# Routed token rows of a mixture layer: a gather by a token table in place of a scatter in sorted order

## What is computed

```python
logits = xf @ gate_w.T                      # xf: 2048 normalized tokens x 512
probs = softmax(logits, axis=-1)            # 8 experts
topk_p, topk_i = top_k(probs, 2)
comb = (one_hot(topk_i, 8) * topk_p[..., None]).sum(axis=1)
h = silu(einsum('nc,eic->eni', xf, w1)) * einsum('nc,eic->eni', xf, w2)
eo = einsum('eni,eci->enc', h, w3)          # 352 hidden features per expert
y = einsum('enc,ne->nc', eo, comb)
sh = silu(xf @ sw1.T) * (xf @ sw2.T) @ sw3.T    # shared expert, 704 hidden
x = x + y + sh
```

## Time and profile before

| | us |
|---|---|
| timed runs, median of 3 | 1809.57 |
| timed runs, lowest and highest | 1806.09 and 1809.67 |
| the profiled execution, first to last instruction (span) | 1828.4 |
| the profiled execution's own time with what lies around the span | not listed |

### The profile page before, as it was taken

The page is one execution under the profiler, slowest core; times in us unless marked ns, Lnnn a source line. Parts: engine busy times, 40 slices in busy tenths (PEclk is TensorE's granted clock), DMA queues, the critical chain, the costliest instruction groups (busy, mean ns, idle before and its releaser), DMA issues.

```text
span 1828.4 us, 26550 instructions
## 1 busy us (share of the span) xinstructions
PE 1714.7 (94%) x9753; PEld 1320.4 (72%) x9753; DVE 1210.7 (66%) x2477; ACT 917.2 (50%) x1937; POOL 183.6 (10%) x299
## 2 busy tenths in 40 slices
PE   5899999999999999998999999998995999999998
PEld 4788888888888888875533333333894999999997
DVE  6665766666655666667689999995541256666756
ACT  2544444444444444332477787877420146666641
POOL 1000000000000000020122322221106000000025
PEclk8999999999999999997799999999897999999999
DMA  4000000010000000022133344442104067887836
GB/s 150 1 1 12 24 24 1 1 35 1 24 1 24 12 24 1 1 59 68 45 96 89 123 141 134 132 135 66 50 13 184 1 231 266 299 273 275 294 122 228
DMA packets 103204, 167.21 MB, mean 91 GB/s; under 512 B 8325, under 2 KB 52357, under 8 KB 102309
## 3 DMA queue, kind: packets, MB, share of 16 engines
q1 hardware_dynamic: 97956, 148.74, 25.3%
q0 software_dynamic: 5120, 16.78, 2.7%
HBM read 116.15 MB, written 49.28 MB: 90 GB/s over the span
## 4 chain that ended last, share of the span: by engine, by line
PE 77%; DVE 16%; issue 3%; ACT 2%; another core or an unknown queue 1%; POOL 1%; DMA 0%; POOLq 0%; DVEq 0%; ACTq 0%
PE ps L189 38%; DVE xmax L1768 9%; PE ps L195 8%; PE ps L1436 7%; PE ps L1239 7%; PE ps L1131 6%; PE ps L1321 4%; PE ps L1192 3%; PE ps L1311 2%; DVE stats L206 1%; PE ps L1372 1%; DVE al L1783 1%; PE ps L1129 1%; ACT ah L1541 1%
## 5 line engine op out<-in xcount | busy, mean ns | idle before, releaser
L1768 DVE TENSOR_REDUCE xmax<-ps 128x1 f32<-128x512 f32 x512 | 320.7, 682 | 36.1 <-PE ps L1192 35.4
L1563 ACT ACTIVATE xp<-ps 128x512 f32<-128x512 f32 x512 | 273.1, 602 | 93.5 <-PE ps L1311 92.5
L1496 ACT ACTIVATE probs<-ps,nmax 128x128 f32<-128x128 f32 (+3 forms) x256 | 136.2, 532 | 164.5 <-DVE nmax L1736 164.5
L1192 PE MATMUL ps<-k,q 48*128 48x512 f32 x512 | 207.3, 483 | 7.4 <-DVE xmax L1768 4.7
L1311 PE MATMUL ps<-q,k 50*128 50x512 f32 x512 | 196.9, 467 | 6.0 <-ACT xp L1563 6.0
L1192 PEld LDWEIGHTS ps<-k,q 48*128 48x128 f32 x512 | 86.7, 193 | 144.7 <-DVE xmax L1768 115.0
L1536 ACT CAST pth<-ps 128x128 fp32r<-128x128 f32 (+3 forms) x256 | 108.5, 424 | 87.7 <-PE ps L195 87.7
L1321 PE MATMUL ps<-xp,vx 128*32 128x512 f32 x1024 | 140.3, 622 | 0.8 <-issue 0.8
L1736 DVE TENSOR_REDUCE nmax<-ps 128x1 f32<-128x128 f32 (+3 forms) x256 | 123.4, 482 | 14.9 <-PE ps L1131 13.5
L189 PE MATMUL ps<-w12h,x_h 128*128 128x352 f32 x568 | 121.6, 336 | 10.8 <-issue 10.3
L1775 DVE TENSOR_TENSOR ptl<-ps,pth 128x128 fp32r<-128x128 f32 (+3 forms) x256 | 123.8, 484 | 2.0 <-ACT pth L1536 2.0
(11 more groups left out here) (191 smaller groups left out, 3527.1 us busy)
## 6 DMA issues: line engine op xcount, KB each, us to landing
w_raw<-in_w_t SPq DMA_DIRECT2D x56, 704.0 KB, 5.9
w_raw<-in_w_t SPq DMA_DIRECT2D x28, 768.0 KB, 5.9
q<-q_way SPq DMA_DIRECT2D x64, 192.0 KB, 3.1
rows_x<-w_raw SPq DMA_DIRECT2D x39, 256.0 KB, 3.3
mixed<-rows_x SPq DMA_DIRECT2D x39, 256.0 KB, 4.3
rows_y<-y_s SPq DMA_DIRECT2D x39, 256.0 KB, 5.5
q_way<-q_hi SPq DMA_DIRECT2D x32, 256.0 KB, 4.2
w_raw<-in_w_qkv_t SPq DMA_DIRECT2D x24, 256.0 KB, 2.9
```

Source lines behind the costliest of these rows:

```text
L1192: pe.matmul(ps[:, bank, :], q3[rows, m % 4, h // 2, i * P:(i + 1) * P].bitcast(F32R), k3[rows, m % KV, :].bitcast(F32R), start=True, stop= ...
L1496: act.activation(probs[u % 4][:, 0:w], ps[:, S_BANK + u % 2, 0:w], ACT.Exp, bias=nmax[:, u % 4:u % 4 + 1], accum_out=rsum[:, u % 4:u % 4 + ...
L1563: act.activation(xp[:, m % 2, h, t, :], ps[:, XST + n % 3, :], ACT.Exp, scale=X_SCALE).then_inc(s_xe, 1)
L1768: dve.tensor_reduce(xmax[:, m % 2, h % 2, h // 2, i:i + 1], ps[:, bank, :], AX_X, ALU.max, negate=True).then_inc(s_xmax, 1)
```

## The change

The scatter goes, and with it `rows_x`, the blanking on SP, the memset on POOL and the semaphores between them. Instead:

- SP stores the 16 tiles of `fn_all` plainly to `rows_n` in DRAM, in token order (`keep_normal`), each after its normalization and spaced by the steps of PE.
- `places` also splits each sorted row number into its tile (number / 128) and its row in the tile (number mod 128), as floats.
- `row_ones` (DVE, in step 7) makes from these two kinds of one-hots: `tile_hot`, 128 x 16 x 40 for each pick, and `row_hot`, 128 x 16 x 128 for each pick. POOL multiplies `tile_hot` by the token numbers. They lie where `y_s`, `fn` and `mixed` lie later.
- `whose_rows` (PE, at the end of step 8) adds 32 products of them into one bank: the token number of each of the 4992 sorted rows, 0 for a row that no token has. DVE copies it as integers in step 9 (`whose_row`).
- POOL gathers each routed tile from `rows_n` into `mixed` by that table (39 indirect DMAs), each once the tile four places ahead has been turned.

The gather at the end and the output are the same.

```diff
@@ SP
-            def take_rows(q):
-                if q >= 4:
-                    sp.wait_ge(s_ft, HEAD_TILES + q - 4 + 1)
-                sp.dma_start(mixed[:, q % 4, :], rows_x[row_of(q):row_of(q) + P, :]).then_inc(s_xr[q % 4], 16)
...
-            def blank(q):
-                if q == 0:
-                    sp.wait_ge(s_zero, 1)
-                sp.dma_start(rows_x[q * P:(q + 1) * P, :], w3_raw[0][:, 0, :]).then_inc(s_blank, 16)
+            def keep_normal(t):
+                sp.wait_ge(s_fn, t + 1)
+                if t >= 2:
+                    sp.wait_ge(s_h1, t // 2)
+                sp.dma_start(rows_n[t * P:(t + 1) * P, :], fn_all[:, t, :]).then_inc(s_kept, 16)
...
             for which in range(3):
                 load_piece(which, 1)
+            for t in range(TILES):
+                keep_normal(t)
             sp.wait_ge(s_tab, 1)
-            sp.wait_ge(s_sort, 16 * TOP * TILES)
-            for q in range(2):
-                take_rows(q)
+            sp.wait_ge(s_kept, 16 * TILES)
             sp.wait_ge(s_ft, HEAD_TILES)
@@ POOL
+            pool.wait_ge(s_ids, 4)
+            for r in range(TOP):
+                pool.wait_ge(s_thot, r + 1)
+                pool.tensor_tensor(tile_hot[:, r], tile_hot[:, r].bitcast(F32),
+                                   tok_f[:, :].unsqueeze(2).to_broadcast([P, TILES, N_WHOSE]), ALU.mult)\
+                    .then_inc(s_tok, 1)
-            pool.wait_ge(s_place, 1)
-            pool.wait_ge(s_blank, 16 * N_ROUTED)
-            pool.wait_ge(s_fn, TILES)
-            for t in range(TILES):
-                for r in range(TOP):
-                    pool.indirect_dma_start(rows_x, bass.IndirectOffsetOnAxis(ap=place[:, r, t:t + 1], axis=0),
-                                            fn_all[:, t, :], None).then_inc(s_sort, 16)
+            pool.wait_ge(s_idx, 1)
+            pool.wait_ge(s_kept, 16 * TILES)
+            for q in range(N_ROUTED):
+                if q >= 4:
+                    pool.wait_ge(s_ft, HEAD_TILES + q - 4 + 1)
+                at = row_of(q) // P
+                pool.indirect_dma_start(mixed[:, q % 4, :], None, rows_n,
+                                        bass.IndirectOffsetOnAxis(ap=whose[:, at:at + 1], axis=0))\
+                    .then_inc(s_xr[q % 4], 16)
@@ PE
+            def whose_rows():
+                pe.wait_ge(s_rhot, TOP)
+                pe.wait_ge(s_tok, TOP)
+                ins = products(pe, whose_ps, [(row_hot[:, r, t, :], tile_hot[:, r, t, :])
+                                              for r in range(TOP) for t in range(TILES)])
+                ins.then_inc(s_who, 1)
...
                 if i == RANK_STEP:
                     ranks()
+                if i == RANK_STEP + 2:
+                    whose_rows()
@@ DVE
-                dve.tensor_copy(place[:, :, :], place_f[:, :, :]).then_inc(s_place, 1)
+                count.seal(dve, dve.tensor_copy(place[:, :, :], place_f[:, :, :]))
+                count.mark(dve.tensor_scalar(part_i[:, 0], place[:, :, :], P - 1, None, ALU.bitwise_and))
+                count.seal(dve, dve.tensor_scalar(part_i[:, 1], place[:, :, :], P.bit_length() - 1, None,
+                                                  ALU.logical_shift_right))
+                dve.tensor_copy(part_f[:, :, :, :], part_i[:, :, :, :]).then_inc(s_row, 1)
+            def row_ones():
+                square, tall = [P, TILES, P], [P, TILES, N_WHOSE]
+                dve.wait_ge(s_ids, 4)
+                dve.wait_ge(s_row, 1)
+                for r in range(TOP):
+                    dve.tensor_tensor(tile_hot[:, r], part_f[:, 1, r, :].unsqueeze(2).to_broadcast(tall),
+                                      steps_f[:, 0:N_WHOSE].unsqueeze(1).to_broadcast(tall), ALU.is_equal)\
+                        .then_inc(s_thot, 1)
+                for r in range(TOP):
+                    dve.tensor_tensor(row_hot[:, r], part_f[:, 0, r, :].unsqueeze(2).to_broadcast(square),
+                                      steps_f[:, :].unsqueeze(1).to_broadcast(square), ALU.is_equal).then_inc(s_rhot, 1)
+            def whose_row():
+                dve.wait_ge(s_who, 1)
+                dve.tensor_copy(whose[:, :], whose_ps).then_inc(s_idx, 1)
...
                 if i == RANK_STEP:
                     places()
+                if i == RANK_STEP + 1:
+                    row_ones()
                 if i == RANK_STEP + 2:
                     slots()
+                if i == RANK_STEP + 3:
+                    whose_row()
```

More of the change, by code:

```diff
@@ L325 @@
 SORTED = N_ROUTED * P
+N_WHOSE = N_ROUTED + N_ROUTED % 2
 THRESHOLDS = BATCH * SEQ // BIG
@@ L338, with row_of @@
 COLUMN = {s: n for n, s in enumerate(BIG_AT + SMALL_AT)}
+def row_of(q):
+    s = FFN[X_FIRST[HEAD_TILES + q]].load - 2
+    col, second = COLUMN[s], q - tiles_of(s)[0]
+    return col * BIG + second * P if col < N_BIG else N_BIG * BIG + (col - N_BIG) * P
 Step = namedtuple("Step", "x load y opens closes")
@@ L522, in build @@
         s_lb = sem("s_lb")
-        s_zero = sem("s_zero")
-        s_blank = sem("s_blank")
         s_num = sem("s_num")
+        s_ids = sem("s_ids")
+        s_kept = sem("s_kept")
+        s_row = sem("s_row")
+        s_rhot = sem("s_rhot")
+        s_thot = sem("s_thot")
+        s_tok = sem("s_tok")
+        s_who = sem("s_who")
+        s_idx = sem("s_idx")
         s_pick = sem("s_pick")
         s_rank = sem("s_rank")
-        s_place = sem("s_place")
         s_tab = sem("s_tab")
-        s_sort = sem("s_sort")
         s_xr = [sem(f"s_xr{n}") for n in range(4)]
@@ L649, in build @@
         xg = sbc("xg", [P, 2, KC, P])
+        with ExitStack() as come:
+            tile_hot = come.enter_context(nc.sbuf_tensor("tile_hot", [P, TOP, TILES, N_WHOSE], F32R))
         y_s = sbc("y_s", [P, Y_RING, HID])
         fn = sbc("fn", [P, TAIL_TILES, HID])
+        with ExitStack() as come:
+            row_hot = come.enter_context(nc.sbuf_tensor("row_hot", [P, TOP, TILES, P], F32R))
         mixed = sbc("mixed", [P, 8, HID])
@@ L689, in build @@
         gate_s = sbc("gate_s", [P, KC, EXPERTS])
+        steps_i = sbc("steps_i", [P, P], mybir.dt.int32)
+        steps_f = sbc("steps_f", [P, P])
+        tok_i = sbc("tok_i", [P, TILES], mybir.dt.int32)
+        tok_f = sbc("tok_f", [P, TILES])
+        part_i = sbc("part_i", [P, 2, TOP, TILES], mybir.dt.int32)
+        part_f = sbc("part_f", [P, 2, TOP, TILES])
+        whose = sbc("whose", [P, N_WHOSE], mybir.dt.int32)
         weights_1 = block_of_weights(1)
@@ L697, in build @@
         rank_ps = ps[:, RANK, 0:EXPERTS * (TILES + 1)]
-        rows_x = nc.dram_tensor("rows_x", (SORTED, HID), F32).ap()
+        whose_ps = ps[:, RANK, 2 * P:2 * P + N_WHOSE]
+        rows_n = nc.dram_tensor("rows_n", (BATCH * SEQ, HID), F32).ap()
         rows_y = nc.dram_tensor("rows_y", (SORTED, HID), F32).ap()
@@ L867, in _ @@
                             context(n + 1)
-                for q in (2 * (m - KV - 1), 2 * (m - KV - 1) + 1):
-                    if 0 <= q < N_ROUTED:
-                        blank(q)
                 if m >= ITEMS - 2:
                     load_piece(m - (ITEMS - 2), 0)
-            sp.wait_ge(s_blank, 16 * N_ROUTED)
             load_piece(2, 0)
@@ L886, in _ @@
                 load_piece(which, 2)
-            for q in range(2, 4):
-                take_rows(q)
             for i in range(N_FFN + 2):
-                for q in range(4, N_ROUTED):
-                    if X_FIRST[HEAD_TILES + q - 4] == i + 1:
-                        take_rows(q)
                 for load in range(RING, N_LOAD):
@@ L1021, in cross @@
                 b, kv = m // KV, m % KV
-                if m == KV:
-                    pool.wait_ge(s_res, GROUPS * TILES + 1)
-                    pool.memset(w3_raw[0][:, 0, :], 0.0).then_inc(s_zero, 1)
                 if m + 1 < ITEMS:
@@ L1054, in _ @@
             power(BATCH - 1, 3 * BATCH)
+            pool.iota(steps_i[:, :], pattern=[[1, P]], base=0, channel_multiplier=0).then_inc(s_ids, 1)
+            pool.iota(tok_i[:, :], pattern=[[P, TILES]], base=0, channel_multiplier=1).then_inc(s_ids, 1)
+            pool.wait_ge(s_ids, 2)
+            pool.tensor_copy(steps_f[:, :], steps_i[:, :]).then_inc(s_ids, 1)
+            pool.tensor_copy(tok_f[:, :], tok_i[:, :]).then_inc(s_ids, 1)
             pool.iota(num_i[:, :], pattern=[[1, N_BIG]], base=0, channel_multiplier=0).then_inc(s_num, 1)
```

## The result

The changed kernel takes 1820.94 us in the median of 5 runs (1819.72 to 1822.43), the kernel before 1809.57 us (1797.03 to 1811.37). The ratio is 1.0084, 95% interval 1.0057 to 1.011: slower, by more than forecast and outside the range.

What follows compares the result with a forecast made beforehand. TensorE was taken to set the time from the feed-forward part on. Slip 0.1, wait 1.3 and matmuls 3.3 sum to 4.7 us, added to 1809.6 for 1814.3 us; the range was 1803 to 1819.

Steps and rivals of the forecast that it cites:

- The hole: TensorE's 27.5 us loss under the 32 scatters in the first profile; taken to come from recording, absent from timed runs.
- B: Rival: a remnant of the hole under the scatters, up to 10.3 us, is in timed runs; 1804.0 to 1813 us; chance 0.22.
- C: Rival: the 27.5 us hole on TensorE under the scatters is in every run; 1786.8 us, faster; chance 0.14.
- The sum, 4.7 us: Time added on TensorE's path by x_l's slip, the wait for row_hot and the 32 matmuls; bounds 3.0 and 7.0.
- slip by x_l: Three more small operations in places() on VectorE delay x_l, which feeds TensorE's step 8: 0.1 us.
- wait for row_hot: TensorE at the end of step 8 waits for VectorE's last large one-hot: 1.3 us, bounds 0.3 and 2.5.
- 32 matmuls: whose_rows() on TensorE, 40 columns each, at 0.10 us each: 3.3 us, upper bound 4.1.
- Gating behind row_hot "covered": VectorE's gating of step 8 slips to 1375.3, but TensorE needs it only after 1379: no cost.
- Costs taken as zero: Removing blanking and scatter gains 0; plain stores on SP and 39 gathers on GpSimd cost 0.
- D: Rival: late gathers make TensorE wait in the routed stage, 0.3 us in 35 steps; 1825 us; chance 0.07.
- E, no wait,: Rival: no wait in whose_rows(), or blanks cost something after all; 3 us or less, 1811 to 1813; chance 0.05.

Runs made afterwards that it cites:

- e1: The kernel before, run and profiled again with no edit: 1809.08 us, ratio 1.0002.
- e10: The kernel before, unchanged, once more for a third trace: 1809.94 us, ratio 1.0004.
- e3: The changed kernel with whose_rows and its copy two steps later and POOL's products only after both row_hot: 1814.06 us, ratio to before 1.0019.
- e2: The changed kernel with whose_rows and its copy two steps later, nothing else: 1816.17 us, ratio to before 1.0035.
- e4: The kernel before with the 39 blanking stores moved from the cross attention into the attention part: 1809.84 us, ratio 0.9997.
- e8: The changed kernel without one-hots and matmuls; POOL scatters token numbers into a DRAM table that SP loads: 1807.73 us, ratio to before 0.9985.
- e5: The changed kernel with PE's wait for row_hot left at step 8, matmuls and copy two steps later: 1820.94 us, ratio to before 1.0066.
- e7: As e3, with both one-hots in bf16 and the token number split in two, 80 columns per matmul: 1810.62 us, ratio to before 1.0012.
- e6: As e3, with the 32 matmuls in eight fours at the ends of steps 10 to 17: 1813.57 us, ratio to before 1.0026.
- e9: The same kernel as e8, run again: 1807.34 us, ratio to before 0.9995.

## Why the prediction was wrong, point by point

**The hole: right in what it isn't, wrong in the reason.** I took it that the hole under the scatters is not in the timed runs, which e1 and e10 confirm, and so the forecast took nothing off the timed runs. But I laid it on the recording. The timed runs of after are listed with their spans and clocks, and the profiled execution is one of them (1822.29 us with a span of 1820.4), so being recorded alone doesn't bring the hole. Whether something was particular to that first recording isn't known. The lever I used, that at least 18.8 us had to be missing from a timed run, was sound; the step to a cause was not. Nor was all of the extra time in two places, as the bound of 10.3 us in B took it. Against e10, whose span is 1808.0, the first profile had 28.1 us more under the scatters and 4.0 us more behind the last routed turn, and it was 11.6 us ahead at the gate's weights; within 0.1 us that gives the 20.4 between the spans, with none of the hole left in e10. B and C fell: e1 and e10 show no remnant, and no timed run is long enough for the whole.

**The sum, 4.7 us: this is the step that failed.** The three terms against what they measured:

| term | forecast | measured | why |
|---|---|---|---|
| slip by x_l | 0.1 | about 0.1 | |
| wait for row_hot | 1.3 (0.3 to 2.5) | 3.1 | row_hot 3.35 us, not 2.29 |
| 32 matmuls | 3.3 (to 4.1) | 6.35 | half clock; 3.5 at full clock |
| half clock in step 9 | 0 | 2.1 | not in the sum |

Together 11.65, of the 12.0 on the ruler. The stated bounds of the sum, 3.0 and 7.0, are also wider than its own terms give, 0.1 + 0.3 + 3.3 = 3.7 and 0.1 + 2.5 + 4.1 = 6.7; no bound allowed for another clock. *The wait:* the slope of the earlier trace rows was right to the last hundredth (2.29 forecast, 2.284 in e3). What I left out is that POOL's products run beside it. I placed them "hidden" and checked only that they end in time, not what they do to the operation they run beside; that is 2 x 1.07 = 2.1 us, which is the excess of the wait over the forecast, 1.8 us, and a little more. The same holds for POOL itself: 1.3 us each was right alone, not beside DVE. *The clock:* I priced a wait at its length and the matmuls at full clock. The rows ahead of the prediction already held the warning: four matmuls that take 0.81 us take 1.10 at the end of the hole. With full clock, the wait at 3.1 and the matmuls at 3.5, the sum would be 6.7 us; the clock adds 2.85 + 2.1 = 4.95, the largest part of what was missed.

**Gating behind row_hot "covered".** True in the changed kernel, where whose_rows holds PE for longer. In e2 it costs 0.99 us. A cover named in a prediction can be the very thing that an improvement removes.

**Costs taken as zero.** Blanking (e4), the scatter (e1 and e10, where PE is busy all through it), the 16 plain stores and the 39 gathers (e8) show no cost, as forecast. Gathers land in 5.4 us in the median where plain loads took 4.3, with over 19 us of lead, and PE is busy for 200 of 200 us from 1500 to 1700 in both kernels. D fell.

**E, no wait,** fell as well. The sign was right, slower; the size was short by more than half. The profiled span did not come near 1806 either: it is 1820.4 - 1805.6 = 14.8 us above. The sum explains 7.3 of it; the gate's weights came 12 us later than in the first profile, which is no work of the change (last section), and the 4.0 us behind the routed turns of that profile were gone.

## What to carry to other kernels

A wait of an engine whose clock follows its work can cost its length and then the half clock behind it: 2.9 us became 5.7 here (e5), while the waits of 0.99 us in e2 and 0.46 in e7 had full clock right behind them. So put a small job's consumer two steps later than you think it needs, and spread narrow matmuls instead of issuing them in a block. Before calling work on another engine hidden, ask what it does to the instruction beside it, not only when it ends. And if a profile's span is longer than every timed run, take a second profile before explaining what it shows.

## What the runs showed of the hardware

- A block of narrow matmuls alone can lower the granted clock without any idle time: 32 fp32r matmuls of 40 columns in 3.5 us, then 0.50 for about 3 us (e3); in fours between wide ones it stays at 1.00 (e6), and so it does behind 32 bf16 matmuls of 80 columns in 1.2 us (e7).
- DVE with two inputs in SBUF and POOL reading SBUF hinder each other: 2.28 us became 3.35 for row_hot, and the durations fit turns in whole instructions.
- The end of the cross attention differs from one execution to the next, and the granted clock with it. In the first profile of before the gate's weights are issued at 1287.05, in e1 at 1295.86, in the changed kernel at 1299.00. The stretch from 1258 to 1293 in the first profile of before, with the clock at 0.94:

```profile
1258.00:1293.00 35.00, 27.32 (x170) 12.29 (x171) 10.73 (x26) 21.25 (x41) 4.33 (x7) 0.94 0.34 105
```

and in the changed kernel, with 0.72:

```profile
1258.00:1293.00 35.00, 30.95 (x149) 9.64 (x149) 8.80 (x22) 20.84 (x40) 3.60 (x6) 0.72 0.21 65
```

The same kernel meets both kinds: the gate's weights are issued at 1292.25 in e8 and at 1287.95 in e9, the same kernel, and at 1287.05, 1295.86 and 1298.62 in the three profiles of the kernel before. About 7 us of it arise behind the last move of the maxima, from which it is 24.9 us to the gate's weights in the first profile of before and in e9, and 31.8 in e1, e10 and the changed kernel. That is of the size by which the kernel before scatters, from 1797 to 1812.6 us, and is the likely cause of it; what tips the clock isn't shown. e10 and the changed kernel are a pair with the same start, 1298.62 and 1299.00: their spans are 1808.0 and 1820.4 us, 12.4 apart; 0.4 of it is the later start, and the ruler says 12.0. The five runs of the changed kernel lie as close as 1819.7 to 1822.4, with no short one among them. That is nothing unusual: only 10 of the 103 runs of the kernel before were below 1805 us.
